# An attention and experts kernel on one core: row maxima spread over the whole group, and half of the operand copies sent mid-group

## The reference

```python
q = split_heads(x @ Wq.T + bq)
k = split_heads(x @ Wk.T + bk)
v = split_heads(x @ Wv.T + bv)
q_lr = jnp.einsum('bhtd,hdr->bhtr', q, Wq_lsr)
k_lr = jnp.einsum('bhtd,hdr->bhtr', k, Wk_lsr)
scores = jnp.einsum('bhir,bhjr->bhij', q_lr, k_lr) * scale
scores = jnp.where(causal_mask, jnp.float32(-jnp.inf), scores)
attn = jax.nn.softmax(scores, axis=-1)
y = jnp.einsum('bhij,bhjd->bhid', attn, v)
```

## Time and profile before

| | us |
|---|---|
| median of the three runs | 3999.77 |
| the profiled execution | 4006.51 |
| its span, first to last instruction | 4004.8 |
| slots 0, 1, 2, 3 and the tail of the third batch | 51.5, 52.3, 60.2, 52.1, 56.8 |

### The profile page before, as it was taken

One profiled execution on the slowest core, in us unless ns is written; L12 is line 12 of the kernel. 1 busy time (PEld: TensorE's weight loads), 2 busy tenths in 40 slices (PEclk: granted clock), 3 DMA queues, 4 the chain that ended last, 5 costly groups with the idle time before them and its releaser, 6 DMA issues. The chain is left out here.

```text
span 4004.8 us, 56465 instructions
## 1 busy us (share of the span) xinstructions
PE 3661.8 (91%) x20457; PEld 2508.7 (63%) x20457; DVE 2291.9 (57%) x5022; ACT 1476.8 (37%) x2763; POOL 658.8 (16%) x852
## 2 busy tenths in 40 slices
PE   4899999999999999999999716799999999999995
PEld 3555555555555555555555306688888888888884
DVE  2576665765665666656657376344544444445456
ACT  1243443443444434434434302333333333333335
POOL 2022121121121221211211200011111111111113
PEclk7999999999999999999999855899999999999997
DMA  5134233233433351433233200433444333334458
GB/s 164 43 106 133 60 96 117 50 105 101 107 81 88 88 143 49 107 106 74 82 101 75 75 0 6 145 117 121 124 128 123 119 117 116 121 117 128 123 167 307
DMA packets 188919, 423.54 MB, mean 106 GB/s; under 512 B 39840, under 2 KB 42912, under 8 KB 180512
## 3 DMA queue, kind: packets, MB, share of 16 engines
q1 hardware_dynamic: 162032, 367.97, 29.9%
q0 software_dynamic: 14400, 35.14, 4.4%
q10 hardware_dynamic: 12288, 17.83, 1.5%
HBM read 246.75 MB, written 72.38 MB: 80 GB/s over the span
## 5 line engine op out<-in xcount | busy, mean ns | idle before, releaser
L795 ACT ACTIVATE probs<-scores_t 128x512 f32<-128x512 f32 (+3 forms) x1536 | 662.3, 497 | 618.3 <-PE scores_t L665 564.9
L1717 PE MATMUL m_ps_h<-m_tokens_t,m_w_parts 128*128 128x512 f32 x3072 | 740.6, 391 | 1.6 <-DVE m_tokens_t L1599 1.6
L1717 PE MATMUL m_ps_y<-m_w_parts,m_hidden_parts 128*128 128x512 f32 x3072 | 737.4, 390 | 0.6
L1717 PEld LDWEIGHTS m_ps_y<-m_w_parts,m_hidden_parts 128*128 128x128 f32 x3072 | 575.4, 188 | 125.8 <-issue 6.2
L1717 PEld LDWEIGHTS m_ps_h<-m_tokens_t,m_w_parts 128*128 128x128 f32 x3072 | 576.1, 188 | 120.3 <-issue 2.0
L851 DVE CUSTOM_DVE_ANT_0 shared_banks<-shared_banks,mask_q_rows 128x128 f32<-128x128 f32 (+3 forms) x1024 | 478.9, 514 | 252.5 <-PE shared_banks L622 247.3
L622 PE MATMUL shared_banks<-k_operands,q_operands 96*128 96x512 f32 (+3 forms) x1536 | 501.9, 385 | 42.5 <-DVE max_slots L851 17.9
L665 PE MATMUL scores_t<-q_operands,k_operands 128*128 128x512 f32 (+3 forms) x1536 | 489.2, 376 | 35.1 <-ACT probs L795 27.0
L622 PEld LDWEIGHTS shared_banks<-k_operands,q_operands 96*128 96x128 f32 x1536 | 280.0, 191 | 302.1 <-issue 115.3
L1535 ACT ACTIVATE m_hidden<-m_ps_h,m_b 128x512 f32<-128x512 f32 x256 | 176.6, 690 | 792.1 <-PE m_ps_h L1717 779.0
L528 POOL TENSOR_SCALAR_AFFINE_SELECT probs<-probs 128x256 f32<-128x256 f32 x512 | 219.9, 432 | 1374.7 <-ACT probs L795 1373.9
(11 more groups left out here) (218 smaller groups left out, 3211.9 us busy)
## 6 DMA issues: line engine op xcount, KB each, us to landing
m_w_raw<-in_w1T SPq DMA_DIRECT2D x64, 1024.0 KB, 5.2
m_w_raw<-in_w2T SPq DMA_DIRECT2D x64, 1024.0 KB, 7.5
q_operands<-natural SPq DMA_DIRECT2D x384, 128.0 KB, 2.5
k_operands<-natural SPq DMA_DIRECT2D x384, 128.0 KB, 2.5
wqk_group<-scratch_wqk SPq DMA_DIRECT2D x32, 1024.0 KB, 6.0
natural<-in_xT SPq DMA_DIRECT2D x8, 2048.0 KB, 9.5
x_residual<-in_x ACTq DMA_DIRECT2D x64, 256.0 KB, 2.9
scratch_x<-probs SPq DMA_DIRECT2D x64, 256.0 KB, 2.2
```

The lines of the kernel that those rows point to most:

```text
L795: act.activation(probs[:, slot_of(k, h // 2), h % 2, c0:HALF], st[:, (HG * k + h) % SCORE_BANKS, c0:HALF], ACT.Exp, scale=SCALE).then_inc( ...
L1717: mm = pe.matmul(bank, a, b, start=(first and n == 0), stop=(final and n == len(pairs) - 1))
```

## The change

**Order of the maxima.** In slots 0 to 2 the pieces of all four heads' first 512 queries (16 pieces, "lower") come first, then the other 32; they start behind part 0 instead of part 9. Slot 3 keeps the order and table of before.

**Halved copies.** In slots 0 and 1 of each batch the projections stand behind parts 27, 42, 56 and 57 instead of 46, 47, 56 and 57. They are now in the order query lower, key lower, query upper, key upper (in every slot). The lower halves of the strips are copied as soon as their projection is done and the scores no longer read that half: 12 DMAs of 32x512 for the query and 12 for the key, in the middle of the slot. The upper halves follow at the slot's end, again 24 DMAs, of 32x512. `load_w` stays behind them.

**Waits.** PE waits for the lower copies (two semaphores, one per two heads) at the first lower piece of heads 0 and 2, and for the other copies at the first upper piece of each head. The reciprocals of a group's second half move from behind parts 0, 4, 4, 5 of the next slot to behind 2, 6, 10, 14, in slots 1 and 2.

```diff
-def max_steps():
+def max_steps(g):
+    lower = [[(h, it, it, 0, (it + 1) * P) for it in range(4)] for h in range(HG)]
+    upper = [[(h, it, it, 0, HALF) for it in range(4, TT)] +
+             [(h, it + 4, it, HALF, (it + 1) * P - HALF) for it in range(4, TT)] for h in range(HG)]
+    if g < GROUPS - 1:
+        return sum(lower, []) + sum(upper, [])
+    return sum((lower[h] + upper[h] for h in range(HG)), [])
...
+MAX_EARLY = (1, 1, 0, 2, 0, 2, 2, 1, 0, 0, 2, 1, 0, 0, 0, 3, 0, 0, 1, 1,
...
+MAX_AFTER = (MAX_EARLY,) * 3 + (MAX_LATE,)
-PROJ_AFTER = (46, 47, 56, 57)
+PROJ_AFTER = ((27, 42, 56, 57),) * HALVED + ((46, 47, 56, 57),) * 2
+LOWER_READ_AT = (3, 7)
-INVERT_AFTER = ((30, 42, 45, 45), (0, 4, 4, 5))
+INVERT_AFTER = ((((30, 36, 42, 45), (2, 6, 10, 14)),) * 3 + (((30, 42, 45, 45), (0, 4, 4, 5)),))
...
+            def lower_strips(b, slot):
+                g = (slot + AHEAD) % GROUPS
+                for i, (ops, order) in enumerate(((q_ops, Q_STRIPS), (k_ops, K_STRIPS))):
+                    await_parts(sp, sp_passed, b, slot, parts=(i,))
+                    plain(sp, st_full, ((b * GROUPS + slot) * NE + LOWER_READ_AT[i] + 1) * HG, sp_passed)
+                    for h in range(HG):
+                        src = slice(DH * h, DH * h + DH)
+                        for s in range(3):
+                            dst = slice(DH * s, DH * s + DH)
+                            sp.dma_start(raw(ops[dst, g % 2, h, 0:HALF]), nat[src, 2 * i + order[s], 0:HALF]
+                                         ).then_inc(lower_sent[h // 2], 16)
...
-                for slot in range(GROUPS - AHEAD):
-                    strips(b, slot)
+                for slot in range(HALVED):
+                    lower_strips(b, slot)
+                    strips(b, slot, first=HALF)
                     if more or slot + 1 < GROUPS - AHEAD:
                         load_w((slot + AHEAD + 1) % GROUPS)
...
-                        if item[2] % 12 == 0:
-
+                        if it == 0 and not lead and 1 <= g <= HALVED and h % 2 == 0:
+                            pe.wait_ge(lower_sent[h // 2], (b * HALVED + g) * LOWER_STRIPS)
+                        if it == (4 if not lead and 1 <= g <= HALVED else 0):
                             pe.wait_ge(strips_sent[h], (1 if lead else nxt + g + 1) * STRIPS)
```

More of the change, by code:

```diff
@@ L174, in attend_steps @@
     return [(hh, j, max(0, j * P - hh * HALF)) for hh in range(2) for j in range(4 * hh + 4)]
-def max_steps():
[L180 to L185, removed]
+def max_steps(g):
[5 more added lines that the diff above has]
+    return sum((lower[h] + upper[h] for h in range(HG)), [])
+N_MAX = 12 * HG
+LOWER_PIECES = 4 * HG
+HALVED = 2
 PROB_BUFS = 4
@@ L226, in plan_slot @@
             order += [("values", g, part[1]), ("sums", g, part[1])]
-        order += [("proj", g, i) for i, at in enumerate(PROJ_AFTER) if at == n]
-        order += [("invert", g, 0, i) for i, at in enumerate(INVERT_AFTER[0]) if at == n]
+        order += [("proj", g, i) for i, at in enumerate(PROJ_AFTER[g]) if at == n]
+        order += [("invert", g, 0, i) for i, at in enumerate(INVERT_AFTER[g][0]) if at == n]
         if g > 0:
-            order += [("invert", g - 1, 1, i) for i, at in enumerate(INVERT_AFTER[1]) if at == n]
-        order += [("max", g, i) for i in range(done, done + MAX_AFTER[n])]
-        done += MAX_AFTER[n]
+            order += [("invert", g - 1, 1, i) for i, at in enumerate(INVERT_AFTER[g][1]) if at == n]
+        order += [("max", g, i) for i in range(done, done + MAX_AFTER[g][n])]
+        done += MAX_AFTER[g][n]
         if n == JOIN_AFTER:
             order.append(("maxT", g))
-    assert done == len(max_steps())
+    assert done == N_MAX
     return order
@@ L331, in build_attention @@
         sp_passed, pool_passed, dve_passed = sem("sp_passed"), sem("pool_passed"), sem("dve_passed")
+        lower_sent = [sem(f"lower_sent{r}") for r in range(2)]
         strips_sent = [sem(f"strips_sent{h}") for h in range(HG)]
@@ L344, in build_attention @@
         STRIPS = 16 * 2 * len(Q_STRIPS)
-        steps, maxes = attend_steps(), max_steps()
-        NE, NM = len(steps), len(maxes)
+        LOWER_STRIPS = STRIPS * HG // 2
+        steps, maxes = attend_steps(), [max_steps(g) for g in range(GROUPS)]
+        NE = len(steps)
         batch = plan_batch()
@@ L400, in seen_by, with await_parts @@
             return (last_seen if b == NB - 1 else batch_seen)[item]
-        def await_parts(eng, passed, b, g, lead=False):
+        def await_parts(eng, passed, b, g, lead=False, parts=(2, 3)):
             _, at, off = scope(b, lead)
-            for i in (2, 3):
+            for i in parts:
                 bank, turn = at[("proj", g, i)]
@@ L421, in load_x @@
                     sp.wait_ge(strips_sent[h], n * STRIPS)
+                for half in lower_sent:
+                    sp.wait_ge(half, n // GROUPS * HALVED * LOWER_STRIPS)
                 sp.dma_start(nat[:], xT_dram.rearrange("(c p) t -> p c t", p=P)[:, :, bass.ds(b * T, T)]
@@ L427, in load_w, with strips @@
                 sp.dma_start(raw(wqk[:]), scratch["wqk"][g].rearrange("p (k c n) -> p k c n", k=4, c=DC)).then_inc(w_in, 16)
-            def strips(b, slot, lead=False, heads=range(HG)):
+            def lower_strips(b, slot):
[9 more added lines that the diff above has]
+                                         ).then_inc(lower_sent[h // 2], 16)
+            def strips(b, slot, lead=False, heads=range(HG), first=0):
                 g = (slot + AHEAD) % GROUPS
@@ L720, in run @@
                         g, i = item[1], item[2]
-                        which, hh = i // 2, i % 2
+                        hh, which = i // 2, i % 2
                         act.wait_ge(bank_full[bank], off[bank] + turn + 1)
@@ L728, in run @@
                                 act.wait_ge(x_split, 2 * (b + 2))
+                            if not lead and g > 0:
+                                for half in lower_sent:
+                                    act.wait_ge(half, (b * HALVED + min(g, HALVED)) * LOWER_STRIPS)
                             if not lead or g == GROUPS - 1:
```

39 lines of the change are left out of this document (21 added, 18 removed).

## The result

The changed kernel takes 4017.36 us (median of six runs, 4013.24 to 4021.42), the kernel before beside it 4001.09 (six runs, 3998.81 to 4001.82): a ratio of 1.0041 with a 95% interval of 1.0028 to 1.0054, so it is slower, by 11 to 22 us. 4012 was forecast, with a range of its own of 4003 to 4024. The profiled execution took 4018.52 us, 12.0 more than the one before.

A forecast was written before the change was run, and what follows sets the result against it. PE was taken as the bound. 8 x (-1.5) for slot 0, 8 x 4.95 for slot 1, 7 x (-2.0) for slot 2 and -1.3 for the last batch gave +12.3 on 3999.8: 4012 us, range 3966 to 4038.

The forecast's parts named there:

- The weights' wait: Slot 1, first projection behind part 27: PE stops 4.85 us for weights landing at +21.1, 3.75 us later than before.
- part 1: Start of slots 0 to 2: maxima between the first eight scores; in slots 1 and 2 net 1.1 us gained by part 27.
- The clock: Slot 1, after the pause for the weights: a lower granted clock costs 1.6 us, between 0 and 3.3.
- what was gained behind the projection: Slot 1, after the first projection: 25 pieces remain instead of 28, DVE and ACT have caught up: -0.4 us.
- Rival C: Slot 1: PE waits but the clock does not fall; slot 1 costs 3.35 us, total 3999 us; chance 0.19.
- Slot 0: Maxima moved into PE's hole at the slot's start gain 1.5 us, between 0.5 and 1.8.
- Slot 2: Four fewer pieces fall where DVE has no time left: 2.0 us gained, 0 to 3; 1.3 in the last batch.
- Slot 3, tail and experts do not change: Slot 3 of each batch, the tail and the experts were forecast to stay as they were.
- each change between kinds of product: On PE, among the moved maxima: some 0.07 us for each change; three more by part 27 cost 0.2 or 0.3.
- Rival A: Slot 1: SP's issue follows the bytes, 0.32 us a copy, so no wait for weights; 3961 us; chance 0.17.
- Rival B: Slot starts: DVE becomes the bound, slot 0 gains 0.5 and slot 2 1.0; 4028 us; chance 0.14.
- The lower copies in mid-slot: Slots 0 and 1: 24 more issues on SP, 15.4 us, cost nothing; slot 0's last key copy there at about +49.

The follow-up runs named there:

- the filled pause: The changed kernel with 20 more products of 512 columns, result unread, ahead of slot 1's first projection and its wait for the weights: 4023.26 us.
- part 1 alone: The kernel before with only the early maxima and spread first-half reciprocals, in slot 0 alone; copies and projections unchanged: 3987.03 us, ratio 0.9972.
- the weights-first kernel: The changed kernel with the load of the weights issued ahead of the 24 upper copies of slots 0 and 1: 3941.52 us, 0.9856 of the kernel before.

## Why the prediction was right, step by step

**The weights' wait** decided, as forecast, and each of its parts can be read off. Issue of a half-size copy: taken 0.6 us, measured 0.59. Weights there at +21.1: measured +20.5 to +21.9 over the eight slots. The wait: 4.85 forecast, 5.34 in the slot shown, 45.1 / 8 = 5.6 by the waits. PE came to it earlier than was forecast, at +15.34 and not +16.25: part 1 had gained 2.0 us by then instead of 1.1, the upper part of its range, since the spread reciprocals let the maxima through. But in front of a wait with a fixed end such a gain is worth nothing.

**The clock** was mis-sized: taken 1.6, measured 2.24 by the filled pause in the slot shown and 2.0 on average. In the batch shown the projection begins 20.68 - 17.35 = 3.33 us behind the place where step 5 ended before, and slot 1 grew by 5.4 = 3.33 + 2.24 - 0.2, against a forecast of 4.95; the 0.2 is what was gained behind the projection, where 0.4 was taken. Rival C (no fall of the clock) is out.

**Slot 0**: -1.5 forecast, -1.58 measured, -1.66 with part 1 alone. The range's bound of 1.8 holds.

**Slot 2**: -2.0 forecast, -3.08 measured; in the last batch -3.0 against -1.3. The reason given stands in the window (DVE busy for 7.75 of 10 us instead of all ten) and in PE's waits for DVE, which are gone; its size was too small by a third.

**"Slot 3, tail and experts do not change"** did not hold: the experts lost 4.3 us and the last slot of all 2.0. That slot in the trace before and after:

```profile
2202.15:2236.97 34.82, 32.39 (x244) 13.30 (x240) 8.16 (x10) 20.82 (x50) 9.60 (x19) 0.97 0.05 16
```

```profile
2208.91:2245.69 36.78, 34.15 (x244) 13.68 (x240) 8.16 (x10) 20.82 (x50) 9.56 (x19) 0.91 0.05 15
```

The work is the same and the granted clock lower; why it fell for longer was not followed up. The errors cancel: 8 x 0.56 in slot 1 + 4.3 + 2.0 on one side, 7 x 1.08 + 1.7 in slot 2 on the other, and the span moved by 12.0 where 12.3 was forecast. That it came so close is luck. By the medians the change is 16.3 us: the run of the kernel before that was traced lies 5.4 above its median (4006.51 against 4001.09), the changed kernel's 1.2. Much of the 5.4 is one slot 1 of 55.35 us; against the other seven, 52.1 on average, slot 1 got 5.9 longer, and the forecast of 4.95 was too small by a sixth.

**Smaller terms.** The 0.07 us taken for each change between kinds of product stands in none of the rows shown. The earlier trace rows show one change, from a score to weighted sums, that costs 761.50 - 761.14 - 0.24 = 0.12 us; between scores and maxima, the changes that part 1 adds, the trace before shows on average no more than between two products of one kind.

**Rival A** is out by its own test, the copies' distance: 0.63 us against the 0.45 at which it would begin. Its sum for the time without the wait, 3961, agrees with 3961.42 for the projection moved behind part 36, but by luck: the experts lose some 4 us in the one and nothing in the other, and slot 2 gains 3.3 instead of 2.0. With the weights first, where PE meets no wait behind part 27 either, the time is 3941.52. **Rival B** (DVE bound at the starts) did not come about, and the spread reciprocals are why, as their return on the weights-first kernel showed (55 us). The prediction costed that edit at nothing and named POOL as what it might delay; what it does for DVE's bank release was not priced. The lower copies in mid-slot cost nothing, as said: no engine waits for them. In slot 0 the last of them lands at +44.9, earlier than the +49 that was taken.

## What to carry to other kernels

When a consumer is moved forward, move what it waits for as well: here a change of 16 us to the bad became one of 57 to the good by issuing one load 24 queue entries earlier. Whether that load may overtake depends on who needs the others (the same edit cost 78 us without the early copies). And behind a pause (here 5.3 us) the dense work that follows pays again, at the lower clock (here 2.0 us in twelve products).

## What the runs showed of the hardware

**The issue of a copy of 32 rows costs the same at 64 and at 128 KB.** The upper copies take 0.59 us each as the whole ones did; halving the bytes did not free the queue.

**The place of a loop's code costs time.** With 96 instructions more ahead of it, the experts' loop has waits for issue of 4 to 5 us, with 152 it has 22, with 256 none; the instruction queue moves 173 packets instead of 118 where it stalls, 2.83 MB / 173 = 16.4 KB each. They are as many with 96 as with 152, so the packets do not tell how long the waits are. The Trainium skill (Advanced Engine Details and Errata, ISA Cache) says that the instruction cache has lines of 16 KB, 256 instructions, and holds 128 KB on TensorE. The packet's size and the return at 256 agree with the line; how many lines the loop occupies was not tried.

**A DMA ahead in the queue slows those behind it, not only by its issue.** The 2 MB input lands in 7.4 us instead of 10.2 when no load of weights was issued right before it, and 128 KB copies in 4.3 instead of 2.5 when one was. Copies of half the size recover within the burst: behind the weights the first of the 64 KB copies lands in 5.2 us, the twelfth in 2.0 again (medians of the eight slots 1 of the weights-first kernel), as all of them do in the changed kernel.
